# A vision tower on one core: softmax scratch read back in four groups of heads, with one reciprocal of the sums

## The reference, cut to what matters

```python
dots = jnp.einsum('bhid,bhjd->bhij', q, k) * scale
attn = jax.nn.softmax(dots, axis=-1)
attn = jnp.einsum('bhij,hg->bgij', attn, reattn_w)
mean = jnp.mean(attn, axis=1, keepdims=True)
var = jnp.var(attn, axis=1, keepdims=True)
attn = (attn - mean) * jax.lax.rsqrt(var + LN_EPS)
attn = attn * ln_gamma[None, :, None, None] + ln_beta[None, :, None, None]
out = jnp.einsum('bhij,bhjd->bhid', attn, v)
```

## Time and profile before

| | |
|---|---|
| median of 3 runs | 852.46 us (850.26 to 853.55) |
| the profiled execution | 854.99 us, span 853.2 us |
| busy: PE, DVE, ACT, POOL | 691.6, 566.3, 436.1, 212.2 us |
| busy share of the DMA engines on SP's queue | 27.0% |
| mean granted clock of TensorE | 0.93 |

### The profile page before, as it was taken

How to read it: one execution, slowest core, us unless ns; L and a number is a source line. 1 busy time by engine, 2 the same in 40 slices (tenths; PEclk the granted TensorE clock), 3 DMA queues, 4 the chain that set the end, 5 groups by cost and what they waited for, 6 DMA issues and landing times.

```text
span 853.2 us, 18885 instructions
## 1 busy us (share of the span) xinstructions
PE 691.6 (81%) x7618; PEld 483.0 (57%) x7634; DVE 566.3 (66%) x1215; ACT 436.1 (51%) x1231; POOL 212.2 (25%) x399
## 2 busy tenths in 40 slices
PE   0859758997889978998899888987899789757654
PEld 0546545766567646765576656764676567535421
DVE  0596647566876788568956786678767885559333
ACT  0103706583566657473748354755666574738311
POOL 0307224102430154014411233024301540033000
PEclk9959967999799999999999979999999999979977
DMA  8400560047102531145005610362025301450000
GB/s 317 159 1 6 176 240 2 1 147 250 40 3 77 187 141 33 45 157 203 33 15 173 216 32 2 112 232 93 2 79 198 129 8 50 152 202 10 1 12 1
DMA packets 42395, 83.98 MB, mean 98 GB/s; under 512 B 3003, under 2 KB 6596, under 8 KB 41668
## 3 DMA queue, kind: packets, MB, share of 16 engines
q1 hardware_dynamic: 41268, 79.29, 27.0%
q10 hardware_dynamic: 1040, 3.49, 1.0%
HBM read 46.98 MB, written 35.79 MB: 97 GB/s over the span
## 4 chain that ended last, share of the span: by engine, by line
PE 39%; DVE 21%; DMA 21%; ACT 10%; issue 6%; POOL 2%; SPq 1%; POOLq 0%; ACTq 0%; DVEq 0%
DMA pg<-turned 12%; DMA turned<-pst 8%; PE big L546 7%; PE small L546 7%; PE big L563 6%; PE small L707 4%; DVE var L1246 4%; DVE an L1290 3%; ACT pst L941 3%; PE small L692 2%; PE big L640 2%; PE small L662 2%; ACT ot L1029 2%; ACT sqb L961 2%; DMA tok_b<-in_tok_b 2%
## 5 line engine op out<-in xcount | busy, mean ns | idle before, releaser
L941 ACT ACTIVATE pst<-big,nb 128x256 f32<-128x256 f32 x256 | 117.9, 474 | 32.0 <-DVE nb L1214 32.0
L1211 DVE TENSOR_REDUCE mx<-big 128x4 f32<-128x1024 f32 x64 | 78.3, 1223 | 52.3 <-PE big L563 51.6
L640 PEld LDWEIGHTS big<-pst,pg 64*64 64x64 f32 x4096 | 72.8, 149 | 52.5 <-DVE an L1290 28.3
L640 PE MATMUL big<-pst,pg 64*64 64x64 f32 x4096 | 80.6, 236 | 21.9 <-DVE an L1290 12.2
L961 ACT ACTIVATE sqb<-big 128x1024 f32<-128x1024 f32 x64 | 65.2, 1020 | 35.7 <-PE big L640 33.8
L1246 DVE TENSOR_REDUCE var<-sqb 128x64 f32<-128x1024 f32 x64 | 77.4, 1211 | 7.5 <-ACT sqb L961 7.5
L1290 DVE TENSOR_TENSOR an<-big,rstd 128x1024 f32<-128x1024 f32 x64 | 78.4, 1224 | 2.2
L662 PE MATMUL small<-w_qkv,xnv 128*128 128x512 f32 x128 | 69.9, 672 | 8.5 <-DVE h L1383 5.7
L563 PE MATMUL big<-qk_t 64*128 64x256 f32 x512 | 72.6, 402 | 3.8 <-ACT qk_t L924 3.7
L692 PE MATMUL small<-an,v 128*64 128x130 f32 (+1 forms) x768 | 56.6, 289 | 21.2 <-ACT ot L1029 20.6
L546 PE MATMUL small<-xnt,w_qkv 128*128 128x256 f32 x256 | 63.8, 392 | 0.0
(11 more groups left out here) (201 smaller groups left out, 1262.8 us busy)
## 6 DMA issues: line engine op xcount, KB each, us to landing
turned<-pst SPq DMA_DIRECT2D x128, 257.0 KB
pg<-turned SPq DMA_DIRECT2D x16, 2056.0 KB, 11.0
w_qkv<-in_w_qkv SPq DMA_DIRECT2D x1, 3072.0 KB
xt<-in_x_t SPq DMA_DIRECT2D x8, 256.0 KB, 2.9
xr<-in_x_tok SPq DMA_DIRECT2D x8, 256.0 KB, 2.7
out<-h SPq DMA_DIRECT2D x16, 128.0 KB
an<-in_gate_t ACTq DMA_DIRECT2D x1, 1024.0 KB, 8.6
an<-in_up_t ACTq DMA_DIRECT2D x1, 1024.0 KB, 10.9
```

The source lines that it names most:

```text
L640: last = mm(mix_place(n)[half[0]:half[1], k_hi * 512 + i * 64:k_hi * 512 + (i + 1) * 64], pg[rows, ib, j], w_rows[rows, it, ib, :], start= ...
L941: last = A(pst[:, g % 2, h % GH, it * T:(it + 1) * T], big[p % 2][:, (j * TT + it) * T:(j * TT + it + 1) * T], ACT.Exp, bias=nb[:, h, it:i ...
L1211: V.reduce_max(mx[:, hs, :], big[p % 2][:, :].rearrange("p (h t l) -> p h t l", h=2, t=TT), AX)\
```

## The change

`turned` is laid out as query group, head within a group of four, group g, place, value. The writes go out pair by pair as before. The read is made in four DMAs, one for each group g of four heads: it waits for the four writes of its group only, and lands on every fourth partition of `pg` (g, g+4, ...), all 16 places at once. On SP's queue the order is: writes of group 0; writes of group 1, read of group 0; writes of group 2, read of group 1; writes of group 3, read of group 2; read of group 3. The rows of the mixing weights (`mix_rep`) are permuted to match.

DVE waits for all four reads and makes one reciprocal of 128x32 in place of two of 128x16; it stands after `ffn_quant` of the second tile. PE waits for all four reads at mixture 0. On POOL the power of the second tile's norm goes ahead of the copy to `hold`; the weights of row tile 0 (two instructions) follow that copy, and the weights of row tile 1 go behind the gain and bias of `mixer_out`.

```diff
+            def spread(b, g):
+                if not is_(b, 0):
+                    sp.wait_ge(s_pg[g], 16 * b)
+                for p in (2 * g, 2 * g + 1):
+                    sp.wait_ge(dve_s.sem, dve_s.at(b, ("tot", p)))
+                    for j in (2 * (p % 2), 2 * (p % 2) + 1):
+                        sp.dma_start(turned[:, j, g, :, :], pst[:, g % 2, j, 0:SUM + TT])\
+                            .then_inc(s_sh[g % 2][p % 2], 16)
+            def gather(b, g):
+                if g == 0:
...
+                for s in s_sh[g % 2]:
+                    sp.wait_ge(s, 16 * 2 * (b * (NGRP // 2) + g // 2 + 1))
+                sp.dma_start(pg[g:P:NGRP, :, 0:SUM + TT], turned[:, :, g, :, :].rearrange("q j i m -> (q j) i m"))\
+                    .then_inc(s_pg[g], 16)
             def regroup(b):
...
+                for g in grps:
+                    spread(b, g)
+                    if g:
+                        gather(b, g - 1)
+                gather(b, NGRP - 1)
```

```diff
-                if do_scores:
-                    row_scales(b + 1, 0)
                 ffn_norm(b, ff, P, 1)
                 ffn_quant(b, ff, P, 1)
+                if do_scores:
+                    row_scales(b + 1)
                 ffn_out(b, ff, P, 0)
-                if do_scores:
-                    row_scales(b + 1, 1)
                 if do_mixer:
                     mixer_out(b + 2)
```

```diff
+                power(b, ff["pool"], ff["dve"], ve_f, rs_f, P, slice(1, 2), ("ve", 1))
                 if do_scores:
                     keep(b + 1)
-                power(b, ff["pool"], ff["dve"], ve_f, rs_f, P, slice(1, 2), ("ve", 1))
-                if do_scores:
-                    scale_weights(b + 1)
+                    scale_weights(b + 1, 0)
                 if do_mixer:
                     mixer_out(b + 2)
+                if do_scores:
+                    scale_weights(b + 1, 1)
```

More of the change, by code:

```diff
@@ L264, in build @@
         s_xr = sem("s_xr")
-        s_pg = [sem(f"s_pg{hf}") for hf in range(2)]
+        s_pg = [sem(f"s_pg{g}") for g in range(NGRP)]
         s_sh = [[sem(f"s_sh{slot}{part}") for part in range(2)] for slot in range(2)]
@@ L314, in build @@
         pool_s = stage("pool_s", ["pcc"])
-        dve_w = stage("dve_w", [0, 1])
-        pool_w = stage("pool_w", [(it, hf) for hf in range(2) for it in range(TT)])
+        dve_w = stage("dve_w", ["rg"])
+        pool_w = stage("pool_w", [(it, hf) for it in range(TT) for hf in range(2)])
         r_order, sq_order, a_order = [], [("sq", 0), ("ln", 0), ("ex", 0), "qs", "cs", ("sq", 1)], [("v", 0)]
@@ L389, in load @@
                     sp.dma_start(xt[:], t["x_t"][b]).then_inc(s_xt, 16)
-            def regroup(b):
[L394 to L414, removed]
+            def spread(b, g):
[8 more added lines that the diff above has]
+                if g == 0:
+                    if is_(b, 0):
+                        sp.wait_ge(setup_pe.sem, setup_pe.at(0, "z"))
+                    else:
+                        sp.wait_ge(pe_r.sem, pe_r.at(b - 1, ("r", NMIX - 1)))
+                for s in s_sh[g % 2]:
+                    sp.wait_ge(s, 16 * 2 * (b * (NGRP // 2) + g // 2 + 1))
+                sp.dma_start(pg[g:P:NGRP, :, 0:SUM + TT], turned[:, :, g, :, :].rearrange("q j i m -> (q j) i m"))\
+                    .then_inc(s_pg[g], 16)
+            def regroup(b):
+                for g in grps:
[3 more added lines that the diff above has]
+                gather(b, NGRP - 1)
             def store(b):
@@ L440, in _ @@
             regroup(0)
-            gather(0)
             load(2)
@@ L629, in mix_heads @@
                         pe.wait_ge(act_o.sem, act_o.at(b - 1, ("o", 1, NO - 1)))
+                if n == 0:
+                    for s in s_pg:
+                        pe.wait_ge(s, 16 * (b + 1))
                 if jt == 0:
-                    if it == 0:
-                        pe.wait_ge(s_pg[hf], 16 * (b + 1))
                     pe.wait_ge(pool_w.sem, pool_w.at(b, (it, hf)))
@@ L1234, in scores, with row_scales @@
                 V.tensor_copy(pckt[:, 0:T], bank[2][0:H, 0:T]).then_inc(dve_s.sem, 1)
-            def row_scales(b, hf):
-                dve.wait_ge(s_pg[hf], 16 * (b + 1))
+            def row_scales(b):
+                for s in s_pg:
+                    dve.wait_ge(s, 16 * (b + 1))
                 if not is_(b, 0):
-                    dve.wait_ge(pool_w.sem, pool_w.at(b - 1, (TT - 1, hf)))
-                ibs = slice(hf * (IB // 2), (hf + 1) * (IB // 2))
-                V.reciprocal(rg[:, :, ibs], pg[:, ibs, SUM:SUM + TT].rearrange("p i t -> p t i")).then_inc(dve_w.sem, 1)
+                    dve.wait_ge(pool_w.sem, pool_w.at(b - 1, (TT - 1, 1)))
+                V.reciprocal(rg[:], pg[:, :, SUM:SUM + TT].rearrange("p i t -> p t i")).then_inc(dve_w.sem, 1)
             def variance(b, n):
@@ L1686, in _ @@
             mixer_values(1)
-            scale_weights(0)
+            scale_weights(0, 0)
             mixer_out(1)
+            scale_weights(0, 1)
             iteration(0, True, True)
```

21 lines of the change are left out of this document (9 added, 12 removed).

## The result

The changed kernel takes **861.12 us** (median of 4 runs, 859.12 to 865.28) for 851.36 (849.25 to 853.55) of the kernel before on the same chip: 1.012 times, interval 1.007 to 1.017. A second measurement of both, at the end of the study, gave 868.81 (6 runs) for 853.69 (17 runs), 1.020 times, 1.016 to 1.024. So the change costs 10 to 15 us. The forecast was 854.0 us, no change, within a range of 845 to 861.

The account below looks back on a forecast made before the run. Bound: the start of rstd 0 after the second residual sum, with DVE nearly gapless from there. Images 1 to 6 +1.8, image 0 +2.0, image 7 -2.3 sum to +1.5 us on 852.46: 854.0 us, range 845 to 861.

Parts of the forecast that it names:

- Part 1: Scratch transfers: early group reads push the last write's landing from 382.4 to 388.2; last read ends at 394.0, before 395.9.
- Part 2: DVE: one reciprocal after the quantisation of x waits about 0.35 us; L1358 can start 1.55 us earlier.
- (a): Last read lands over 5.4 us after the second residual sum starts, DVE waits; 1 us late gives 861; chance 0.22.
- Part 3: POOL: 2.1 us of late weights join the chain; rstd 0 starts 16.2 us after the second residual sum starts.
- The sum: Whole kernel: images 1 to 6 +1.8 us, first image +2.0, last image -2.3, together +1.5 us.
- gain of 1.0 in image 4: Image 4 of the eight: 1.0 us faster, since its late data are no longer waited for.
- Image 0: First image: data 1.9 us earlier, but PE does three mixtures after it; the values of L662 start 2.0 us later.
- image 7: Last image, without mixer work: all data in at 756.3 instead of 758.23, rstd 0 about 764.6 for 766.88, -2.3 us.
- (b): Rival: reads cost writes little and locks bite less; data land at 387 to 391, time 841 to 846; chance 0.24.
- (c): Rival: queue serves early reads only behind all writes, data at 395.9 as now; 865 us; chance 0.04.
- The median: Whole time: +1.5 us, worked out on an execution 2.5 us above the median, applied to median 852.46 gives 854.0.

Follow-up runs that it names:

- the reads alone: Kernel before with only the four group reads; two reciprocals at their old places needing all four reads, POOL in its old order: 875.58 us.
- the write of 128 rows: Scratch laid out head by head, read back in eight DMAs of 16 partitions, order otherwise as in the changed kernel: 1027.41 us.
- the filler: Changed kernel plus 5 and 10 unread matmuls in PE's idle time, before the transposes of quantised h and before mixture 3: 862.03 us.

## Why the prediction failed, step by step

**Part 1, the transfers: right, with one step wrong.** The last write was forecast to land 13.1 us after its issue, and took 12.82 and 13.10 (image 3 of the two profiles); the last read was to take 5.8 and took 5.30 and 5.88. In the clock of before the data would have come at 394.3 and 395.5, well inside the bounds of 387 and 399. What failed is the sentence **"Issues on SP's queue rise by two an image; SP only waits there."** The waits indeed held nothing up: read 1, the last one ahead of the last four writes, was issued at H-17.8, and these writes' data were not ready before H-15.7. But issuing is not free either. The last write left at H-12.8 instead of H-13.8, one microsecond late, because the four issues of the last group, which follow one another without a gap (4.11 us in the timeline above), lasted 0.58, 0.85, 1.27 and 1.26 us; in before the first three took 0.57, 0.57 and 0.62 us, and only the last one 1.48. With the reads all issued late they took 0.57, 0.57, 0.77 and 1.39 us, and the last write left at H-13.6: the longer issues go with the reads that are under way. So the last read could be issued only at H+0.06 and H+0.69, where H-0.7 was forecast. Another 0.2 us pass between the landing and the start of the reciprocal. By the Trainium skill, DMA: Bandwidth & Descriptors, section on why a DMA increments its semaphore by 16, a write of 8 blocks uses eight engines; the share of one half and the write of 128 rows that landed in 3.2 us both agree.

**Part 2, one reciprocal: right in kind, 0.65 us late.** It lasts 0.35 us as forecast. In eleven of twelve images it started after H+5.4, the point that rival (a) named. L1362 stands at H+8.35 on average, not at H+7.7.

**Part 3, POOL: right.** From L1362 to rstd 0 the forecast had 16.2-7.7=8.5 us; measured are 16.74-8.35=8.4. The locks were as priced. The two DVE instructions took 2.80 us for 1.44, the two weights 2.49 for 2.04; the forecast had 404.3-401.45=2.85 from the first one's turn to the second one's end, and 403.75-401.25=2.5 for the weights. By the Trainium skill, SBUF — State Buffer, section Who interferes with whom, tensor_scalar in a 2-port mode and a GpSimd instruction hold each other off for a whole instruction, and a DVE instruction with two inputs in SBUF contends with a GpSimd instruction that reads SBUF; 1.38 for 0.75 us here, and 1.05 for 0.23 us at rstd 0, whose two inputs lie in SBUF, agree.

**The sum: the step that failed.** It made the time of an image follow rstd 0 and nothing else, **"a later rstd 0 moves the mixing, less 0.15 us"**, and gave images 1 to 6 +1.8 us. Measured, as the mean of two profiles, is +9.7. Of the 7.9 that are missing, 5.8-1.8=4.0 are a rstd 0 later than forecast (0.54 us in each image, from the data; and the kernel before stood at H+15.6 to H+16.0 in its second profile, so that the forecast's gain of 1.0 in image 4 was one execution's accident), and 3.9 lie behind rstd 0, where the sum had no term. There the granted clock fell in 11 of 12 images, for 2 of 12 before, and the forecast had nothing for it. What it said of rstd 0 held: a microsecond there moves the image by a microsecond. The rows to see the missing term were at hand: the forecast took the period as about 89 us in all of images 1 to 6, but image 4 of before had its data late, rstd 0 at H+17.0, and an interval of 94.5 us for 89.3 in image 3, so 1.3 us of delay stood beside 5.2 us of loss. And image 1, with the earliest rstd 0 of all (H+15.0), took 92.4 us. Both had a low spell of 10.2 us in the mixing, and both lost 3.9 us behind rstd 0. Why the spells come in nearly every image of the changed kernel stays open: lateness of rstd 0 is not enough, as the reads alone show, with rstd 0 at H+19.0 and no low spell in the mixing, nor is it needed, as image 1 shows.

Image 0 was to cost 2.0 and the beginning cost 1.0; image 7 was to give 2.3, and the end gave 0.7.

**The rivals.** (a), data later than H+5.4 and then a wait on DVE, is what happened, at 0.35 us past its point on average. By its own price, some 8 us for each microsecond, that is 3 us, about 857; that its 861 for a full microsecond is what was measured is luck, for the rest came from the low spells. (b) and (c) did not occur: the data came before H+6.8 in every image of both profiles, and the writes were indeed pushed.

**The median.** The sum was made against one execution of before that had two low spells and lay 2.5 us above the median; to carry +1.5 over to the median supposed that the changed kernel would have low spells as rarely as before. It had them in nearly every image.

## What to carry to other kernels

A transfer that is issued early into a busy queue takes its time from what is already there: here the early reads made the last write land later, and reads issued after the last write came out the same. A wait in the queue, by contrast, cost nothing as long as nothing behind it was due. Work that is moved off one chain must not land between two steps of another, nor beside the short instructions that release it; moving the same 2 us of weights from ahead of rstd 0 to behind it was worth 16 us, low spells included, and made the slower change a faster one. And when images that should be alike differ in one profile, find out by how much each is longer and behind which step before using their mean: the loss behind rstd 0 stood in two images of before, and only one of them was late.

## What the runs showed of the hardware that was not expected

The granted clock differs between executions of the same program: the kernel before had it below 1.00 in the mixing of two images and then of none, spans of 853.2 and 847.2 us, and mean clocks of 0.930 to 0.952 over 80 runs. The wait of PE just ahead of mixture 3 does not decide it by itself: it was 1.69 us in image 3 of the changed kernel (above) and in image 5 as well, and the clock fell only in the first. The wait before that one, for the transposes of the quantised h, was 0.99 us in image 3 and 0.42 us in image 5. With the filler in place the spells showed elsewhere. What decides it is left open.

A DVE instruction of 0.23 us on 64 columns, next to a POOL instruction of 1.02 us, took 1.05 us. An issue of the same write on SP's queue took 0.57 us with little under way, and 1.1 to 1.7 us at the end of a run of writes. And sixteen busy DMA engines can mean 408 or 110 GB/s, with the form of the read.
